# Second attention: both halves of a score tile ahead of the row chunks of their slot

## The chip, the core and the metric

The kernel runs on one core of a Trainium2 chip. TensorE (PE) multiplies, VectorE (DVE), ScalarE (ACT) and GpSimd (POOL) do the rest, and SyncE (SP) issues most DMAs. Each engine works through its own queue in order, and semaphores tie the queues together. The metric is the device time of one execution, in microseconds (us).

## What is computed

A two-layer transformer on x of shape (2, 1024, 256). Each layer is an attention and an MLP, each between layer norms with a residual sum: a 16-head attention in bf16, a mixture of 16 experts, then a "forgetting" attention with 32 heads of 8 in fp32, and an MLP with int8 weights. Only the forgetting attention is touched:

```python
q, k, v = heads of x @ Wq.T, x @ Wk.T, x @ Wv.T          # 32 heads of 8
c = cumsum(log_sigmoid(x @ Wf.T + bf), axis=1)
scores = einsum('bihd,bjhd->bhij', q, k) * scale + (c_i - c_j)
p = softmax(where(causal, scores, -inf))
o = einsum('bhij,bjhd->bihd', p, v) ; return o @ Wo.T
```

## The kernel before, in words

`attention` (L622) works through 32 units; a unit is two heads of one batch (1024 queries, 1024 keys). Each unit needs two passes of score matmuls.

The **row pass** finds the maximum of every query row. `row_chunk` (L680) multiplies a block of 128 queries with up to 512 keys into `row`, a ring of three PSUM buffers (`SLOTS`). DVE takes the maximum (`max_of`, L836: a masked custom operation at L845 for the last chunk of a row, a plain reduction at L849 otherwise) and frees the buffer (`row_free`). A unit has 24 chunks (`CHUNKS`, numbered 0 to 23). When all are through, `turn_max` (L691) transposes the maxima with eight small matmuls into one more `row` buffer, and DVE adds them to the rows of `q_sb` (`add_max`, L863). Chunks and turns are called entries; the entry n waits on PE until DVE has freed the entry n - 3.

The **score pass** makes the transposed, shifted scores. `scores(u, g, part)` (L708) issues one of the two halves of score tile g (two matmuls into `st`, a ring of two PSUM buffers); the second half fires `st_ready`. The first half waits until ACT has done the exp of tile g - 2. ACT does one exp per tile (L791 for the tiles 0 to 7 of one head, L794 for 8 to 11 of both), POOL clears what lies above the diagonal (L819), and `values` (L728) multiplies the probabilities with v into `o`. After the first exp of the next unit ACT copies `o` to `oT` (L779), which waits for the last values.

PE's order is written out by hand. The loop `for k in range(NGR)` has 12 slots a unit. Slot k issues the scores of tile k + 2 (in slots 10 and 11 the tiles 0 and 1 of the next unit), the row entries of `LATER[k]` for the next unit or the one after that, and in the odd slots the values of `VALUES[k]`. `LATER` is ((12, 13), (14, 15), (16, 17), (18, 19), (20, 21), (22, 23), (0, 1), (2,), (TURN, 3), (4, 5, 6), (7, 8, 9), (10, 11)). Before the change a slot is issued as: first half, first entry, second half, other entries, values. The last two units have no unit to prepare, so parts of their slots are empty.

Of the kernel before, what the change touches and what calls it, by code (L numbers as in the profile page):

```python
# [353 lines left out]
def columns_of(kb):  # L354


    at = [POS[qb] for qb in range(kb, TB)]
    return min(at) * P, (max(at) + 1) * P
# [18 lines left out]
def exp_groups():  # L377
# [10 lines left out]
LATER = ((12, 13), (14, 15), (16, 17), (18, 19), (20, 21), (22, 23),  # L388
         (0, 1), (2,), (TURN, 3), (4, 5, 6), (7, 8, 9), (10, 11))
# [232 lines left out]
def attention(nc, tag, units, hd, m_row, dt, load, k_steps, k_sb, v_units, o_rows, mask, ident_b):  # L622
# [11 lines left out]
    with ExitStack() as ctx:  # L634
# [19 lines left out]
        def columns(kb, h):  # L654


            lo, hi = columns_of(kb)
            return (lo, hi, 0) if kb < TB // 2 else (lo, hi, h * SIDE - lo)

        def group_of(kb, h):  # L660

            return 2 * kb + h if kb < TB // 2 else TB + kb - TB // 2

        @block.sync
        def _(sp):
            k_steps(sp, k_sb, steps_loaded)
            for u in range(RING):
                load(sp, u, q_sb[:, u], k_sb[:, u], qk_loaded[u])
            for u in range(units):
                if u and u + 3 < units:  # L670
                    sp.wait_ge(st_ready, NGR * u)
                    load(sp, u + 3, q_sb[:, (u + 3) % RING], k_sb[:, (u + 3) % RING], qk_loaded[(u + 3) % RING])
                sp.wait_ge(o_copied, u + 1)
                sp.dma_start(o_rows[u * 4 * HW:(u + 1) * 4 * HW, :], oT[:, u % 2]).then_inc(stored[u % 2], 16)
            for k in range(2):
                sp.wait_ge(stored[k], 16 * (units // 2))

        @block.tensor
        def _(pe):
            def row_chunk(u, i):  # L680

                qb, h, lo, w = CHUNKS[i]
                n = entry_of[u, i]
                if i == 0:
                    pe.wait_ge(qk_loaded[u % RING], 64 * (u // RING + 1))
                if n >= SLOTS:
                    pe.wait_ge(row_free, n - SLOTS + 1)
                nc.tensor.matmul(row[:, n % SLOTS, 0:w], q_sb[:, u % RING, POS[qb] * P:(POS[qb] + 1) * P],  # L688
                                 k_sb[:, u % RING, h, lo:lo + w], start=True, stop=True).then_inc(row_ready, 1)

            def turn_max(u):  # L691

                n = entry_of[u, TURN]
                pe.wait_ge(m_parts, 3 * (u + 1))
                pe.wait_ge(row_free, n - SLOTS + 1)
                turned = row[:, n % SLOTS].bitcast(BF16)
                for qb in range(TB):
                    last = nc.tensor.transpose(turned[:, POS[qb] * P:(POS[qb] + 1) * P],
                                               mcol[:, u % 2, qb].rearrange("p h r -> p (h r)"), ident_b[:])
                last.then_inc(row_ready, 1)  # L700

            def entry(u, what):
                if what == TURN:
                    turn_max(u)
                else:
                    row_chunk(u, what)

            def scores(u, g, part):  # L708

                kb, heads = GROUPS[g]  # L710
                n = NGR * u + g
                if part == 0:
                    if g == 0:

                        pe.wait_ge(row_free, entry_of[u, TURN] + 1)
                    if n >= 2:
                        pe.wait_ge(exp_done, n - 1)
                lo, hi = columns_of(kb)
                if len(heads) == 1:
                    h, first, end, to = heads[0], max(lo, SIDE * part), min(hi, SIDE * (part + 1)), 0  # L720
                else:
                    h, first, end, to = part, lo, hi, part * SIDE - lo
                last = nc.tensor.matmul(st[:, n % 2, to + first:to + end], k_sb[:, u % RING, h, kb * P:(kb + 1) * P],  # L723
                                        q_sb[:, u % RING, first:end], start=True, stop=True)
                if part == 1:
                    last.then_inc(st_ready, 1)

            def values(u, kb):  # L728

                if kb == 0:  # L730
                    pe.wait_ge(v_ready, u + 1)
                    if u:
                        pe.wait_ge(o_copied, u)
                pe.wait_ge(masked, TB * u + kb + 1)
                for side in range(2):
                    for h in range(2):
                        lo, hi, to = columns(kb, h)
                        first, end = max(lo, SIDE * side), min(hi, SIDE * (side + 1))
                        if first >= end:
                            continue  # L740
                        at = HW * (2 * h + side)
                        last = nc.tensor.matmul(o[at:at + HW, first - SIDE * side:end - SIDE * side],  # L742
                                                v_sb[:, u % RING, kb, h, :],
                                                probs[:, (NGR * u + group_of(kb, h)) % GR, to + first:to + end],
                                                start=(kb == 0), stop=(kb >= TB - 2), skip_group_check=True)
                last.then_inc(pv_done, 1)

            pe.wait_ge(steps_loaded, 32)
            for i in range(NC // 2):
                entry(0, i)  # L750
            for slot in LATER:
                for what in slot:
                    entry(0 if what == TURN or what >= NC // 2 else 1, what)
            for g in range(2):
                for part in range(2):
                    scores(0, g, part)

            for u in range(units):
                for k in range(NGR):
                    to_u, to_g = (u, k + 2) if k + 2 < NGR else (u + 1, k + 2 - NGR)  # L760
                    if to_u < units:
                        scores(to_u, to_g, 0)
                    for m, what in enumerate(LATER[k]):
                        to = u + 1 if what == TURN or what >= NC // 2 else u + 2
                        if to < units:
                            entry(to, what)
                        if m == 0 and to_u < units:
                            scores(to_u, to_g, 1)
                    for kb in VALUES.get(k, ()):
                        values(u, kb)  # L770

# [29 lines left out]
        @block.gpsimd  # L801
        def _(pool):
            def copy_v(u):
                if u >= RING:
                    pool.wait_ge(pv_done, TB * (u - RING + 1))
                nc.gpsimd.tensor_copy(v_sb[:, u % RING, :, :, 0:hd + 1], v_units[:, u]).then_inc(v_ready, 1)

            def causal(u, kb):

                n = NGR * u + group_of(kb, 1)  # L810
                pool.wait_ge(exp_done, n + 1)
                lo, _, _ = columns(kb, 0)
                if kb < TB // 2:
                    first = (n - 1) % GR
                    tiles = probs[:, first:first + 2, POS[kb] * P:(POS[kb] + 1) * P]
                else:
                    at = POS[kb] * P - lo
                    tiles = probs[:, n % GR].rearrange("p (h n) -> p h n", h=2)[:, :, at:at + P]
                nc.gpsimd.affine_select(tiles, tiles, [[0, 2], [1, P]], ALU.is_ge, 0.0, base=0,  # L819
                                        channel_multiplier=-1).then_inc(masked, 1)  # L820

            nc.gpsimd.memset(v_sb[:], 0.0).then_inc(v_clear, 1)
            pool.wait_ge(v_clear, 1)
            copy_v(0)
            for u in range(units):
                if u + 1 < units:
                    copy_v(u + 1)
                for kb in range(TB):
                    causal(u, kb)
# [964 lines left out]
```

## Time and profile before

| | |
|---|---|
| median of 3 runs | 1985.34 us (1984.33 to 1985.52) |
| profiled execution | 1983.64 us, span 1981.9 us |
| PE busy | 1522.3 us, 77% of the span |
| DVE busy | 1310.3 us, 66% |
| ACT busy | 844.9 us, 43% |
| POOL busy | 247.9 us, 13% |
| second attention | about 1221 to 1740 us of the span |

Times in rows are us from the span's start. A timeline row has the start, the length, the engine, the line, the operation, output <- inputs, the shape, and in brackets the idle time of the engine just ahead of it with what ended it. Matmul lengths overlap: what a matmul takes of PE is the distance to the next start. Rows of like instructions next to each other are merged ("x2"), and a few matmul records are missing.

### The profile page before, as it was taken

The numbers are of one execution on the slowest core, as the hardware profiler recorded it, in microseconds if no ns is written. First come the engines' busy times: TensorE is split into PE (matmuls) and PEld (weight loads), VectorE is DVE, ScalarE is ACT, GpSimd is POOL, SyncE is SP. The second block draws the span as 40 slices with busy tenths as digits, with TensorE's granted clock in tenths as the row PEclk, the third lists the DMA queues.
The fourth block names the chain that finished last, engine by engine and source line by source line (L and its number), as shares of the span: only waits on it lengthen the run. The fifth ranks groups of instructions, "written<-read, shape, count | busy, mean of one in ns | idle before, by whom it ended". The sixth has DMA issues, their size and how long they took to land. (4 is left out here: it accounts for less than half of the span.)

```text
span 1981.9 us, 28852 instructions
## 1 busy us (share of the span) xinstructions
PE 1522.3 (77%) x9011; PEld 827.1 (42%) x9088; DVE 1310.3 (66%) x3794; ACT 844.9 (43%) x1534; POOL 247.9 (13%) x409
## 2 busy tenths in 40 slices
PE   3555555542199999999999393999999999963995
PEld 1122222211167777777777261333333333341564
DVE  4888888866445554555455567888888888636543
ACT  3888988860011111111111240566666666623212
POOL 0000000000121121212110110222222222201000
PEclk9555555555599999999999695999999999976998
DMA  2255565651100000000000064111111111020001
GB/s 85 59 103 103 105 104 106 104 115 18 29 24 14 20 22 14 28 14 28 14 19 1 12 241 150 33 54 55 54 49 49 49 49 49 33 61 19 1 1 43
DMA packets 203881, 105.52 MB, mean 53 GB/s; under 512 B 164502, under 2 KB 180886, under 8 KB 203502
## 3 DMA queue, kind: packets, MB, share of 16 engines
q1 hardware_dynamic: 202542, 102.01, 20.8%
q10 hardware_dynamic: 1216, 2.03, 0.4%
q8 instruction: 57, 0.93, 0.2%
q14 instruction: 66, 0.54, 0.1%
HBM read 40.68 MB, written 29.36 MB: 35 GB/s over the span
## 5 line engine op out<-in xcount | busy, mean ns | idle before, releaser
L1221 PE MATMUL moe_gu<-all_xT_bf,moe_parts 128*112 128x512 bf16 x1536 | 344.9, 382 | 17.8 <-POOL moe_parts L1046 17.8
L1258 ACT ACTIVATE moe_th<-moe_gu 112x512 f32<-112x512 f32 x128 | 76.4, 597 | 489.2 <-PE moe_gu L1221 489.2
L791 ACT ACTIVATE a_probs<-a_st 128x1024 f32<-128x1024 f32 (+3 forms) x256 | 212.3, 865 | 158.4 <-PE a_st L723 158.3
L688 PE MATMUL a_row<-l_k,a_q 128*128 128x512 bf16 (+3 forms) x736 | 230.1, 334 | 45.4 <-DMA l_k<-k_rows 27.1
L1221 PEld LDWEIGHTS moe_gu<-all_xT_bf,moe_parts 128*112 128x112 bf16 x1536 | 201.2, 131 | 147.3 <-POOL moe_parts L1046 17.9
L845 DVE CUSTOM_DVE_ANT_0 a_unread<-a_row,all_mask 128x128 bf16<-128x128 f32 (+3 forms) x512 | 238.6, 485 | 32.2 <-PE a_row L688 27.6
L1274 DVE SCALAR_TENSOR_TENSOR moe_tmp<-moe_th,moe_gu 112x512 f32<-112x512 f32 x128 | 88.0, 687 | 255.4 <-ACT moe_th L1258 244.1
L723 PE MATMUL a_st<-a_q,l_k 128*128 128x384 bf16 (+3 forms) x735 | 223.6, 327 | 26.7 <-ACT a_probs L791 24.5
L1235 PE MATMUL moe_dn<-moe_wd,moe_actT 112*128 112x256 f32 x1024 | 231.4, 379 | 0.0
L570 DVE CUSTOM_DVE_ANT_0 a_rows<-a_sc,all_mask 128x128 bf16<-128x128 f32 (+7 forms) x256 | 192.5, 752 | 43.7 <-PE a_sc L493 42.5
L1235 PEld LDWEIGHTS moe_dn<-moe_wd,moe_actT 112*128 112x128 f32 x1024 | 194.7, 190 | 30.2
L849 DVE TENSOR_REDUCE a_mx<-a_row 128x1 f32<-128x512 f32 x256 | 175.9, 687 | 38.6 <-PE a_row L688 38.5
L506 PE MATMUL a_o<-a_v,a_turned_sb 128*128 128x16 bf16 x1152 | 73.6, 179 | 164.1 <-DMA a_turned_sb<-a_rows 163.5
L526 ACT ACTIVATE a_rows<-a_rows 128x128 bf16<-128x128 bf16 (+7 forms) x256 | 173.2, 677 | 40.9 <-DVE a_rows L580 35.9
L493 PE MATMUL a_sc<-a_k,a_q 16*128 16x512 bf16 (+3 forms) x384 | 167.5, 505 | 12.2 <-DVE a_mx L570 7.5
L742 PE MATMUL a_o<-a_probs,a_v 128*32 128x384 f32 (+3 forms) x1920 | 176.7, 432 | 0.0
L506 PEld LDWEIGHTS a_o<-a_v,a_turned_sb 128*128 128x128 bf16 x1152 | 50.6, 106 | 293.7 <-DMA a_turned_sb<-a_rows 265.7
L535 ACT ACTIVATE a_unread<-a_rows 128x128 bf16<-128x128 bf16 (+7 forms) x256 | 170.6, 666 | 0.0
L819 POOL TENSOR_SCALAR_AFFINE_SELECT a_probs<-a_probs 128x256 f32<-128x256 f32 x256 | 102.5, 406 | 412.1 <-ACT a_probs L791 336.1
L723 PEld LDWEIGHTS a_st<-a_q,l_k 128*128 128x128 bf16 x768 | 73.7, 97 | 184.1 <-ACT a_probs L791 112.5
L688 PEld LDWEIGHTS a_row<-l_k,a_q 128*128 128x128 bf16 x768 | 75.1, 98 | 124.1 <-DVE a_mx L849 31.8
L1288 DVE SCALAR_TENSOR_TENSOR all_y<-moe_dn,moe_wcur,all_y 128x256 f32<-128x256 f32 x256 | 111.7, 477 | 15.5 <-PE moe_dn L1235 15.5
(198 smaller groups left out, 1668.1 us busy)
## 6 DMA issues: line engine op xcount, KB each, us to landing
a_q<-q_rows SPq DMA_DIRECT2D x64, 128.0 KB
l_k<-k_rows SPq DMA_DIRECT2D x64, 128.0 KB
o_rows<-a_oT SPq DMA_DIRECT2D x32, 256.0 KB, 2.0
a_turned_sb<-a_rows SPq DMA_TRANSPOSE x256, 2.6
moe_raw<-in_gate SPq DMA_DIRECT2D x16, 224.0 KB, 3.1
moe_raw<-in_up SPq DMA_DIRECT2D x16, 224.0 KB, 3.4
moe_wd<-in_down SPq DMA_DIRECT2D x16, 224.0 KB, 2.8
q_rows<-qkv_parts SPq DMA_DIRECT2D x4, 768.0 KB, 3.6
```

Of the source, the lines that this page charges most:

```text
L493: last = nc.tensor.matmul(sc[:, n % 3, lo // 512, 0:w], q_sb[32 * h:32 * h + hd, u % 2, qb * P:(qb + 1) * P], k_sb[32 * h:32 * h + hd, u % ...
L526: nc.scalar.activation(row, row, ACT.Exp).then_inc(exp_done, 1)
L535: nc.scalar.activation(unread[:, n % 2, 0:w], rows[:, u % 2, at:at + w], ACT.Copy, accum_out=total[:, u % 2, e:e + 1]).then_inc(summed, 1)
L570: nc.vector.tensor_tensor_reduce(out=rows[:, u % 2, at:at + w], in0=sc[:, n % 3].rearrange("p a n -> p (a n)")[:, 0:w], in1=mask[:, S - w: ...
L688: nc.tensor.matmul(row[:, n % SLOTS, 0:w], q_sb[:, u % RING, POS[qb] * P:(POS[qb] + 1) * P], k_sb[:, u % RING, h, lo:lo + w], start=True, ...
L723: last = nc.tensor.matmul(st[:, n % 2, to + first:to + end], k_sb[:, u % RING, h, kb * P:(kb + 1) * P], q_sb[:, u % RING, first:end], star ...
L742: last = nc.tensor.matmul(o[at:at + HW, first - SIDE * side:end - SIDE * side], v_sb[:, u % RING, kb, h, :], probs[:, (NGR * u + group_of( ...
L791: nc.scalar.activation(probs[:, n % GR, lo:hi], st[:, n % 2, lo:hi], ACT.Exp).then_inc(exp_done, 1)
L845: nc.vector.tensor_tensor_reduce(out=unread[:, n % SLOTS, 0:w], in0=tile[:, 0:w], in1=mask[:, at:at + w], scale=1.0, scalar=-3e38, op0=ALU ...
L849: nc.vector.tensor_reduce(top, tile[:, 0:w], mybir.AxisListType.X, ALU.max).then_inc(row_free, 1)
L1221: last = nc.tensor.matmul(gu[0:IC, n % 2, i, :], parts[:, j, k // KC, i, k % KC, ch * IC:(ch + 1) * IC], xT[:, k % KC, g * 512:(g + 1) * 512],
L1235: last = nc.tensor.matmul(dn[:, i, 0:D], actT[:, g % 2, ch, i * P:(i + 1) * P], wd[:, j, ch, :], start=(ch == 0), stop=(ch == 1))
```

## The change

In each slot the second half of the score tile is issued straight behind the first half, ahead of all row entries. What is issued in a slot, and how often, stays the same, and so do the other engines' queues and all waits.

```diff
                     to_u, to_g = (u, k + 2) if k + 2 < NGR else (u + 1, k + 2 - NGR)
                     if to_u < units:
                         scores(to_u, to_g, 0)
-                    for m, what in enumerate(LATER[k]):
+                        scores(to_u, to_g, 1)
+                    for what in LATER[k]:
                         to = u + 1 if what == TURN or what >= NC // 2 else u + 2
                         if to < units:
                             entry(to, what)
-                        if m == 0 and to_u < units:
-                            scores(to_u, to_g, 1)
                     for kb in VALUES.get(k, ()):
                         values(u, kb)
```

## Rows read from the trace of the kernel before

**Rows 1.** Windows: length, busy PE, PEld, DVE, ACT, POOL; PEclk, DMA, GB/s.

```profile
1400.00:1500.00 100.00, 91.45 (x714) 35.83 (x727) 82.66 (x275) 61.97 (x83) 22.05 (x57) 1.00 0.17 56
...
1728.00:1740.00 12.00, 9.79 (x92) 3.15 (x92) 0.00 (x0) 9.73 (x14) 3.20 (x8) 1.00 0.07 25
1740.00:1750.00 10.00, 0.23 (x1) 0.27 (x2) 3.73 (x2) 0.00 (x0) 0.00 (x0) 0.58 0.70 176
```

**Rows 2.** Waits, 1250 to 1730 us: us in total, times, longest.

```profile
PEld a_st L723 <- ACT a_probs L791: 104.7, 121, 1.2
...
ACT a_oT L779 <- PE a_o L742: 28.2, 30, 0.9
PEld a_row L688 <- DVE a_mx L849: 26.3, 60, 0.5
PE a_st L723 <- ACT a_probs L791: 22.5, 30, 0.8
```

**Rows 3.** Timeline of PE, slots 8 and 9 of one unit.

```profile
1266.70 0.61 PE L698 MATMUL a_row<-all_ident_b,a_mcol 128*128 128x128 bf16 x8
1267.15 0.27 PE L723 MATMUL a_st<-a_q,l_k 128*128 128x256 bf16 x1
1267.26 0.22 PE L688 MATMUL a_row<-l_k,a_q 128*128 128x128 bf16 x1
...
1268.10 0.50 PE L688 MATMUL a_row<-l_k,a_q 128*128 128x512 bf16 x2 [0.29 <-DVE a_q L866]
```

**Rows 4.** Timeline of PE and its weight loads (PEld), slots 10 and 11 of the same unit.

```profile
1269.96 0.38 PE L723 MATMUL a_st<-a_q,l_k 128*128 128x512 bf16 x1
1270.18 0.43 PE L688 MATMUL a_row<-l_k,a_q 128*128 128x384 bf16 x2
...
1270.90 0.10 PEld L688 LDWEIGHTS a_row<-l_k,a_q 128*128 128x128 bf16 x1 [0.47 <-DVE a_mx L849]
1270.91 0.39 PE L688 MATMUL a_row<-l_k,a_q 128*128 128x512 bf16 x1 [0.30 <-DVE a_mx L849]
...
1271.38 0.34 PE L688 MATMUL a_row<-l_k,a_q 128*128 128x384 bf16 x1
```

**Rows 5.** Timeline of PE, end of slot 0 and start of slot 1.

```profile
1272.78 0.38 PE L688 MATMUL a_row<-l_k,a_q 128*128 128x512 bf16 x1
1273.91 0.39 PE L723 MATMUL a_st<-a_q,l_k 128*128 128x512 bf16 x1 [0.75 <-ACT a_probs L791]
```

**Rows 6.** Timeline of DVE, the same slots.

```profile
1267.35 0.69 DVE L866 TENSOR_TENSOR a_q<-a_row,a_q 128x1024 bf16<-128x1024 bf16 x1 [0.51 <-PE a_row L698]
...
1270.16 0.69 DVE L849 TENSOR_REDUCE a_mx<-a_row 128x1 f32<-128x512 f32 x1 [0.36 <-PE a_row L688]
...
1271.24 0.08 DVE L845 DVE_READ_ACCUMULATOR2_ANT a_mx<- 128x1 f32 x1
...
1276.25 0.69 DVE L849 TENSOR_REDUCE a_mx<-a_row 128x1 f32<-128x512 f32 x1 [0.90 <-PE a_row L688]
```

**Rows 7.** Timeline of ACT: copies of o 15 units apart, and the exps behind.

```profile
1272.34 0.58 ACT L779 COPY a_oT<-a_o 128x512 f32<-128x512 f32 x1 [0.94 <-PE a_o L742]
1272.82 2.70 ACT L791 ACTIVATE a_probs<-a_st 128x1024 f32<-128x1024 f32 x3
...
1509.74 0.58 ACT L779 COPY a_oT<-a_o 128x512 f32<-128x512 f32 x1 [0.94 <-PE a_o L742]
```

**Rows 8.** Timeline of PE, slots 2 and 3.

```profile
1276.05 0.33 PE L723 MATMUL a_st<-a_q,l_k 128*128 128x384 bf16 x1
1276.21 0.27 PE L688 MATMUL a_row<-l_k,a_q 128*128 128x256 bf16 x1
...
1277.00 0.39 PE L688 MATMUL a_row<-l_k,a_q 128*128 128x512 bf16 x1
```

**Rows 9.** Timeline of DVE and PE, slots 4 and 5: chunks 20 and 23.

```profile
1278.89 0.08 DVE L845 DVE_READ_ACCUMULATOR2_ANT a_mx<- 128x1 f32 x1
...
1279.34 0.22 PE L688 MATMUL a_row<-l_k,a_q 128*128 128x128 bf16 x1
```

## Prediction

> **What bounds the kernel now.** I read the windows first. In the second attention TensorE (PE) is busy 91 of 100 us, DVE 83, ACT 62, at a granted clock of 1.00 [rows 1]. No engine is full, so the waits come next, then the order of instructions in one unit.
>
> The table of waits [rows 2] misleads at its top: the loads for `a_st` (L723) sat idle 104.7 us "for ACT". A load row is idle while the values' matmuls run ahead of it on PE. Of PE proper only 22.5 us, 30 times, waited for ACT, and loads of row chunks waited 26.3 us, 60 times (two a unit), for DVE's reductions.
>
> So I laid out one unit. The copies of `o` to `oT` stand at 1272.34 and 1509.74, 15 units apart: 15.83 us a unit [rows 7]. In these 15.83 us PE's queue, which goes strictly in program order, is stopped at five places. "Chunk i" is entry i of `CHUNKS`, "slot k" one pass of `for k in range(NGR)`.
> 1. Slot 9, chunk 5: waits until DVE has read the turned maxima (`add_max`, L866), since it takes the same `row` buffer. DVE's 1267.35 + 0.69 = 1268.04, PE goes at 1268.10 [rows 3, 6].
> 2. Slot 11, chunk 10: waits for chunk 7's reduction, 1270.16 + 0.69 = 1270.85, PE goes at 1270.91 [rows 4, 6].
> 3. Slot 11, chunk 11: waits for chunk 8, read out at 1271.24 + 0.08 = 1271.32, PE goes at 1271.38 [rows 4, 6].
> 4. Slot 1, first half of group 3: waits for the exp of group 1, which ends about 1.03 after 1272.82; PE goes at 1273.91, against a queue free at 1272.78 + 0.22 = 1273.00: 0.91 us [rows 5].
> 5. Slot 3, chunk 19: waits for chunk 16's reduction, 1276.25 + 0.69 = 1276.94, PE goes at 1277.00 [rows 6, 8].
>
> A release thus costs 0.06 us each time. Everything else is PE issuing without a stop. Wait 4 isn't about scores: group 1's exp starts at 1272.82 because ACT was in the copy of `o` from 1272.34, and the copy had waited for the last values [rows 2, 7], which stand behind chunk 11 on PE. So the unit is one ring of PE issue, PE to DVE to PE hand-offs (1, 2, 3, 5) and one hand-off by way of values, copy and exp (4).
>
> **The change part by part.** No instruction is added or removed, and no DMA, SP or POOL instruction is moved. In each slot the second half of a score tile goes ahead of the slot's first row entry. (a) The second half comes earlier by the first entry's time. (b) The first entry comes later by the second half's time. Later entries and values stay where they were in the queue.
>
> (a) **What comes earlier.** `st_ready` fires 0.06 us (one matmul of 128 columns) to 0.45 us (the turn) sooner [rows 3], so 12 exps a unit can start sooner. PE waits for an exp only at place 4, and that exp starts behind the copy of `o`, not behind its scores: its second half is issued soon after 1270.91, over a microsecond before 1272.82 [rows 4, 7]. The other scores go when the values ahead of them are through. Gain: 0. The earlier exps are paid out as ACT idle time. If this cover were gone, the gain could be wait 4 at most, 0.91 us a unit.
>
> (b) **What comes later.** In nine of twelve slots the delayed chunk is one that nobody waits for: PE reads no `row` result, DVE has a backlog or idle time, and the chunk three entries on is far behind. It decides where a later chunk already waits for DVE's release of it. Those are the places above:
> - Slot 8 holds the turn of the maxima. Its eight transposes go at 1266.70, ahead of the second half of group 10 (256 columns). That half takes 1267.15 to 1267.26 = 0.11 us of PE [rows 3]. Afterwards it is ahead, the turn ends 0.11 later, `add_max` starts 0.11 later (DVE was idle 0.51 us for exactly this [rows 6]), and chunk 5 goes 0.11 later: **+0.11**.
> - Slot 10, chunk 7: the second half (512 columns) takes 1269.96 to 1270.18 = 0.22 us [rows 4]. DVE was idle 0.36 us for chunk 7 [rows 6], so its reduction slips by 0.22. The releases for chunks 10 and 11 slip with it (DVE runs 7, 8, 9 back to back). In slot 11 both halves now go first and then PE stands twice: chunk 10 goes at 1270.91 + 0.33, chunk 11 at 1271.38 + 0.33 (0.33 with the 0.11 of the turn). The values and the copy behind chunk 11, and so wait 4, follow: **+0.22**.
> - Slot 2, chunk 16: the second half (384 columns) takes 1276.05 to 1276.21 = 0.16 us [rows 8]. DVE had been idle 0.90 us for chunk 16 [rows 6]; it and the release for chunk 19 slip. The values of slot 3 stand behind chunk 19: **+0.16**.
> - The next tightest is chunk 23 in slot 5, which needs chunk 20: DVE has read chunk 20 at 1278.89 + 0.08 and 0.06 later is 1279.03, against chunk 23 at 1279.34: 0.31 us to spare, 0.15 after chunk 20's delay by 0.16 (its slot's second half has 384 columns too) [rows 9]. No wait; if that slack were wrong, at most 0.16 more a unit.
>
> The three add, since each shifts the whole ring and no slack lies between: wait 4 moves with the copy, and the table of waits has no line in which PE's values wait for POOL. **0.11 + 0.22 + 0.16 = 0.49 us a unit**, 15.83 to 16.32. The first two happen in the units 0 to 29 (in the last two no chunk follows), the third in 0 to 30: 30 x 0.33 + 31 x 0.16 = 14.9 us.
>
> The profiled execution has 1983.64 us (span 1981.9). 1983.64 + 14.9 = 1998.5, that is +0.75%. It lies 1.7 below the median of the runs, 1985.34, so I add the same there: **2000.2 us**.
>
> Bounds of the unknown. The order "half, half, chunk" has no row in this trace. Nearest are the eight transposes: eight loads and matmuls of 128 columns fit in 1266.70 to 1267.15, 0.056 each [rows 3], so a load hides behind even the shortest matmul: extra cost 0. The far bound is one load of 0.10 us [rows 4] exposed per unit where a wait moved, 3 us in all. Below: one of the three slips absorbed by a slack that I missed, minus 3 to 6 us. I take the sum as it is.
>
> **The rivals.**
> - *Earlier scores pay* (faster). If the exp that PE waits for were released by its scores, the whole wait 4 (0.91 us) could shrink by what the second half of slot 11 moves forward, about 0.47 us a unit, 31 times: -14 us, 1971. For it: the waits table puts PE's waits for ACT first [rows 2]. Against: group 1's exp starts straight after the copy [rows 7]. It decides only if the copy stopped being the releaser.
> - *Nothing happens.* The delayed chunks vanish in DVE's idle time (17 of 100 us [rows 1]): 1985. Against: the idle time lies exactly ahead of the instructions that are delayed [rows 6].
> - *Partly absorbed.* One or two of the three terms count: +5 to +10 us, 1990 to 1995.
> - *A fourth wait*, chunk 23 or exposed loads: 2003 to 2005.
> - *The clock falls.* PE now stands 0.49 us a unit more. The granted clock was 1.00 at 91% busy and still 1.00 in 1728 to 1740 at 82%; it was down only in 1740 to 1750, where PE did almost nothing [rows 1]. I compute 91.45 x 15.83/16.32 = 88.7 busy afterwards, above that 82. A unit at the lower level (1.2 GHz) would take up to some 14 us more, its PE issue time again (15.83 less the stops, an estimate); three units of 32 would give 2042. The Trainium skill has the rule against this change ("TensorE: Matmul & The Clock Gate", section "A second HAM failure mode: psum-queue depth-cycling"): frequent micro-idles between groups of matmuls can make the clock swing between its levels. By that rule the stage would lose tens of us; this trace doesn't bear it out, with its five stops a unit at 1.00 throughout.
>
> **How the numbers follow.** Forecast 0.74, earlier scores pay 0.05, nothing 0.08, partly absorbed 0.08, a fourth wait 0.03, clock 0.02. The range 1994 to 2005 takes in the forecast with its bounds (2000.2 minus one term of 5, plus 0.16 x 31 = 5), the upper part of the partly absorbed case and the fourth wait: about 0.8. Some 0.2% (4 us) is what a measurement of this kernel can tell from no change. Faster 0.05; same 0.08; slower 0.87.
>
> **What would show it.** Period of the copies 16.32 us in place of 15.83. Stage longer by 14.9 us, all else unchanged. Idle of DVE per unit up by 0.49: ahead of `add_max` 0.51 to about 0.62, ahead of chunk 7 0.36 to about 0.58, ahead of chunk 16 0.90 to about 1.06. PE's stops at chunk 10 and chunk 11 both about 0.25 us, at chunk 19 0.14 to 0.30; wait 4 unchanged at 0.91. Exps relative to PE earlier, and ACT's idle time total up by 0.49 a unit all the same. Busy share of PE 89 of 100 us and clock still 1.00. I'd be wrong if DVE's idle gaps grew but the period didn't, if wait 4 shrank, or if a load row stood exposed between the halves.

## The result, and the profile after

The changed kernel takes 2001.32 us (median of 4 runs, 2000.48 to 2002.54) against 1985.43 us: ratio 1.0080, interval 1.0063 to 1.0098, 15.9 us slower. The profiled execution has a span of 1999.1 us against 1981.9. Two single executions of kernels tried below lie far outside all others, one with slot 10 alone (3753.36 us) and one with nine slots (2291.72 us); nothing explains them, and times and ratios leave them out.

First the copies of `o` to `oT` on ACT, as in [rows 7]; these two are 14 units apart.

```profile
1276.47 0.58 ACT L778 COPY a_oT<-a_o 128x512 f32<-128x512 f32 x1 [1.37 <-PE a_o L742]
...
1504.88 0.58 ACT L778 COPY a_oT<-a_o 128x512 f32<-128x512 f32 x1 [1.37 <-PE a_o L742]
```

(1504.88 - 1276.47) / 14 = 16.315, so 16.32 us a unit, as forecast, where it was 15.83. (The lines of the file have moved up by one: L778 is the L779 of before.) ACT stood 1.37 us ahead of the copy in place of 0.94: the exp of the next group 0 was earlier, the values later. ACT got its scores sooner and spent the gain waiting.

PE's timeline of one unit at its stops. 1272.02 (chunks 5 and 6) answers to [rows 3], 1275.05 (chunks 10 and 11) to [rows 4], 1278.04 (both halves of group 3) to [rows 5], 1280.78 (chunks 18 and 19) to [rows 8]:

```profile
1271.24 0.38 PE L688 MATMUL a_row<-l_k,a_q 128*128 128x512 bf16 x1
1272.02 0.50 PE L688 MATMUL a_row<-l_k,a_q 128*128 128x512 bf16 x2 [0.40 <-DVE a_q L865]
...
1274.37 0.38 PE L723 MATMUL a_st<-a_q,l_k 128*128 128x512 bf16 x1
1275.05 0.81 PE L688 MATMUL a_row<-l_k,a_q 128*128 128x512 bf16 x2 [0.30 <-DVE a_mx L848]
...
1276.75 0.54 PE L688 MATMUL a_row<-l_k,a_q 128*128 128x384 bf16 x2
1278.04 0.55 PE L723 MATMUL a_st<-a_q,l_k 128*128 128x512 bf16 x2 [0.75 <-ACT a_probs L790]
1278.43 0.43 PE L688 MATMUL a_row<-l_k,a_q 128*128 128x256 bf16 x2
...
1280.45 0.49 PE L723 MATMUL a_st<-a_q,l_k 128*128 128x384 bf16 x2
1280.78 0.90 PE L688 MATMUL a_row<-l_k,a_q 128*128 128x512 bf16 x2
```

Chunk 5 is stopped with 0.40 idle where it was 0.29. Chunk 10 stands about 0.24: the two halves ahead of it (the record of the second is missing) take 0.22 each from 1274.37, so the queue is free at 1274.81. The pair of chunks 10 and 11 spans 0.81 us; without a stop between them it would be 0.22 + 0.33 = 0.55, so chunk 11 stands about 0.25 as well. The pair of 18 and 19 spans 0.90 where two 512-column chunks in a row take 0.22 + 0.38 = 0.60: chunk 19 stands 0.30, before 0.14. The wait for the exp of group 1 has kept its 0.75 of idle time. Counted from the queue being free, as the prediction counts it, it is 1278.04 - (1276.75 + 0.16 + 0.22) = 0.91, also as before.

DVE in the same unit, as [rows 6]:

```profile
1271.27 0.69 DVE L865 TENSOR_TENSOR a_q<-a_row,a_q 128x1024 bf16<-128x1024 bf16 x1 [0.62 <-PE a_row L698]
...
1274.30 0.69 DVE L848 TENSOR_REDUCE a_mx<-a_row 128x1 f32<-128x512 f32 x1 [0.58 <-PE a_row L688]
...
1277.11 0.56 DVE L844 CUSTOM_DVE_ANT_0 a_unread<-a_row,all_mask 128x384 bf16<-128x384 f32 x1 [0.23 <-PE a_row L688]
...
1280.55 0.69 DVE L848 TENSOR_REDUCE a_mx<-a_row 128x1 f32<-128x512 f32 x1 [0.90 <-PE a_row L688]
```

The idle time ahead of `add_max` grew from 0.51 to 0.62 and ahead of chunk 7 from 0.36 to 0.58. Ahead of chunk 16 it is still 0.90, and there is a new 0.23 ahead of chunk 12 (below).

The waits from 1250 to 1745 us, as [rows 2], and the window that answers to [rows 1]. The first line here is of the kernel before (its waits from 1250 to 1730 us), for the last line of the next fence:

```profile
PE a_row L688 <- DVE a_q L866: 8.8, 30, 0.3
```

```profile
PEld a_st L723 <- ACT a_probs L790: 105.8, 122, 1.2
...
ACT a_oT L778 <- PE a_o L742: 41.2, 30, 1.4
...
PEld a_row L688 <- DVE a_mx L848: 34.5, 60, 0.6
...
PE a_st L723 <- ACT a_probs L790: 22.5, 30, 0.8
...
PE a_row L688 <- DVE a_q L865: 12.1, 30, 0.4
```

```profile
1400.00:1500.00 100.00, 89.98 (x707) 35.88 (x718) 79.98 (x268) 59.93 (x82) 21.98 (x57) 1.00 0.15 48
```

PE's real wait for ACT is 22.5 us before and after. What grew are the waits for DVE: PE's own for `add_max` from 8.8 to 12.1 us (30 x 0.11), and that of the row chunks' loads for DVE's reductions from 26.3 to 34.5. (The latter are load rows, so they show which wait grew and not by how much PE stood.) PE, DVE, ACT and POOL are all less busy, and the granted clock is still 1.00.

### The profile page after: what moved, and what is told of

The parts are those of the page before. It is cut to its first block and busy times, and to the rows that moved or that the text cites. A ratio compares the mean times of both kernels' runs of the same rounds, so it can differ in the third digit from the quotient of the medians.

```text
span 1999.1 us, 28852 instructions
## 1 busy us (share of the span) xinstructions
PE 1528.7 (76%) x9011; PEld 828.1 (41%) x9088; DVE 1307.5 (65%) x3794; ACT 842.9 (42%) x1534; POOL 249.0 (12%) x409
## 5 line engine op out<-in xcount | busy, mean ns | idle before, releaser
L790 ACT ACTIVATE a_probs<-a_st 128x1024 f32<-128x1024 f32 (+3 forms) x256 | 207.6, 867 | 171.3 <-PE a_st L723 171.2
L688 PE MATMUL a_row<-l_k,a_q 128*128 128x512 bf16 (+3 forms) x735 | 201.9, 334 | 50.6 <-DMA l_k<-k_rows 26.9
L723 PE MATMUL a_st<-a_q,l_k 128*128 128x384 bf16 (+3 forms) x736 | 183.4, 329 | 30.9 <-ACT a_probs L790 23.9
L723 PEld LDWEIGHTS a_st<-a_q,l_k 128*128 128x128 bf16 x768 | 55.7, 98 | 166.9 <-ACT a_probs L790 112.5
L1287 DVE SCALAR_TENSOR_TENSOR all_y<-moe_dn,moe_wcur,all_y 128x256 f32<-128x256 f32 x256 | 111.7, 477 | 15.6 <-PE moe_dn L1234 15.5
```

The source lines that it names most:

```text
L790: nc.scalar.activation(probs[:, n % GR, lo:hi], st[:, n % 2, lo:hi], ACT.Exp).then_inc(exp_done, 1)
```

## The experiments

Each is shown with its edit, what was expected of it and the period of a unit from two copies in its trace. The slot sets below are tested in one loop; `TOGETHER` and `CHUNK_FIRST` stand for the sets, which each kernel has written into that line. Unless another set is named, both are empty, which is the order of before:

```diff
+                    together, chunk_first = k in TOGETHER, k in CHUNK_FIRST
-                    if to_u < units:
+                    if to_u < units and not chunk_first:
                         scores(to_u, to_g, 0)
+                        if together:
+                            scores(to_u, to_g, 1)
                     for m, what in enumerate(LATER[k]):
...
-                        if m == 0 and to_u < units:
+                        if m == 0 and to_u < units and chunk_first:
+                            scores(to_u, to_g, 0)
+                        if m == 0 and to_u < units and not together:
                             scores(to_u, to_g, 1)
```

### One slot at a time

Slot 8 alone (`TOGETHER = (8,)`):

> The kernel before, with both halves first in slot 8 alone (the slot of the turn). Theory of three hand-offs: the turn, add_max and chunk 5 go 0.11 us later, nothing else: period of a unit 15.83 + 0.11 = 15.94 us, 30 x 0.11 = +3.3 us. Rival, a small cost in every slot (0.49 / 12 = 0.04 us each, from pairing the halves): period 15.87, +1.3 us. Rival, no effect of this slot (DVE's idle time takes it): 15.83, 0.

```profile
1274.26 0.58 ACT L784 COPY a_oT<-a_o 128x512 f32<-128x512 f32 x1 [0.94 <-PE a_o L742]
...
1513.31 0.58 ACT L784 COPY a_oT<-a_o 128x512 f32<-128x512 f32 x1 [0.94 <-PE a_o L742]
```

239.05 / 15 = 15.94 us. Time 1988.28 against 1985.01, ratio 1.0018 (1.0009 to 1.0028), +3.3 us.

Slot 10 alone (`TOGETHER = (10,)`):

> The kernel before, with both halves first in slot 10 alone (chunk 7). Three hand-offs: chunk 7 goes 0.22 us later, and with it the releases for chunks 10 and 11 and all that follows: period 16.04 us, 30 x 0.22 = +6.5 us. Cost in every slot alike: 15.87, +1.3 us. No effect: 15.83, 0.

```profile
1272.08 0.59 ACT L784 COPY a_oT<-a_o 128x512 f32<-128x512 f32 x1 [1.37 <-PE a_o L742]
...
1512.70 0.59 ACT L784 COPY a_oT<-a_o 128x512 f32<-128x512 f32 x1 [1.37 <-PE a_o L742]
```

240.62 / 15 = 16.04 us. Time 1992.07, ratio 1.0040 (1.0024 to 1.0056), +7.1 us.

Slot 2 alone (`TOGETHER = (2,)`):

> The kernel before, with both halves first in slot 2 alone (chunk 16). Three hand-offs: chunk 16 and the release for chunk 19 go 0.16 us later: period 15.99 us, 31 x 0.16 = +5.1 us. Cost in every slot alike: 15.87, +1.3 us. No effect: 15.83, 0.

```profile
1273.32 0.59 ACT L784 COPY a_oT<-a_o 128x512 f32<-128x512 f32 x1 [0.94 <-PE a_o L742]
...
1513.17 0.59 ACT L784 COPY a_oT<-a_o 128x512 f32<-128x512 f32 x1 [0.94 <-PE a_o L742]
```

239.85 / 15 = 15.99 us. Time 1989.27, ratio 1.0020 (1.0008 to 1.0031), +4.3 us.

The other nine slots (`TOGETHER` = all but 2, 8 and 10):

> The changed kernel with the slots 2, 8 and 10 put back to the old order: both halves first in the nine others. Three hand-offs: period 15.83 us and the time of the kernel before, within 0.1%. Cost in every slot alike: 9 x 0.04 = 0.37 us a unit more, period 16.19, +11 us. Earlier scores pay: below 15.83.

```profile
1274.35 0.58 ACT L784 COPY a_oT<-a_o 128x512 f32<-128x512 f32 x1 [0.94 <-PE a_o L742]
...
1511.77 0.59 ACT L784 COPY a_oT<-a_o 128x512 f32<-128x512 f32 x1 [0.94 <-PE a_o L742]
```

237.42 / 15 = 15.83 us. Time 1986.71, +1.7 us, ratio 1.0007 (0.9997 to 1.0017): no difference clear of noise. The three slots' excess over 15.83 is 0.11 + 0.21 + 0.16 = 0.48 us a unit, the whole change's 0.49, the other nine's 0. So the cost isn't one of pairing the halves, or of loading weights twice in a row; it sits in three slots, in the sizes of the second halves that were put ahead there. DVE in the kernel with the nine slots:

```profile
1274.99 0.56 DVE L850 CUSTOM_DVE_ANT_0 a_unread<-a_row,all_mask 128x384 bf16<-128x384 f32 x1 [0.23 <-PE a_row L688]
...
1278.26 0.69 DVE L854 TENSOR_REDUCE a_mx<-a_row 128x1 f32<-128x512 f32 x1 [0.73 <-PE a_row L688]
```

It stands 0.23 us ahead of chunk 12, which slot 0's second half made late, and makes up for it ahead of chunk 16: 0.73 in place of 0.90. In this kernel the delay is free, since DVE's next idle time takes it up and no stop of PE depends on it in between.

### The wait for the exp of group 1

ACT's copy goes behind the exp of group 1:

```diff
-                    if g == 0 and u:
+                    if g == 1 and u:
                         copy_out(u - 1)
```

> The kernel before, with ACT's copy of o to oT moved from behind the exp of group 0 to behind that of group 1. It takes wait 4 (0.91 us a unit) out of the ring, if that wait was due to the copy and not to the scores. Theory: exp of group 1 starts as its scores are there, PE doesn't stop in slot 1: period 15.83 - 0.91 = 14.92 us, 31 x 0.91 = -28 us. Rival, the scores released that exp: 15.83, 0.

```profile
1269.93 0.58 ACT L784 COPY a_oT<-a_o 128x512 f32<-128x512 f32 x1
...
1508.38 0.58 ACT L784 COPY a_oT<-a_o 128x512 f32<-128x512 f32 x1
```

238.45 / 16 = 14.90 us. Time 1955.61 against 1985.54, ratio 0.9852 (0.9836 to 0.9869), -29.9 us. Nothing about the scores was changed, and 0.93 us a unit went. So the biggest stop of PE was due to the copy, not to late scores.

The same with both halves first in all slots:

> The copy moved as in the other run, and both halves first in every slot as in the changed kernel. Three hand-offs: they cost the same 0.49 us without wait 4: period 14.92 + 0.49 = 15.41 us, 15 us slower than with the moved copy alone. Rival, earlier scores pay once the copy isn't the releaser: as fast as the moved copy alone or faster, 14.92 or below. Rival, wait 4 was needed for the loss to show: the loss shrinks to under 0.3 us a unit.

```profile
1273.42 0.58 ACT L784 COPY a_oT<-a_o 128x512 f32<-128x512 f32 x1 [0.46 <-PE a_o L742]
...
1506.25 0.58 ACT L784 COPY a_oT<-a_o 128x512 f32<-128x512 f32 x1 [0.45 <-PE a_o L742]
```

232.83 / 15 = 15.52 us. Time 1975.35, ratio 0.9949 (0.9932 to 0.9965). Earlier scores don't pay here either; the loss is 0.62 us a unit and 19.7 us in all, more than the 0.49 that I expected. The further 0.13 can be found in the trace. Chunks 14 and 15 in PE's timeline, and DVE's reading of chunk 12:

```profile
1507.28 0.57 PE L688 MATMUL a_row<-l_k,a_q 128*128 128x256 bf16 x2
```

```profile
1506.89 0.56 DVE L850 CUSTOM_DVE_ANT_0 a_unread<-a_row,all_mask 128x384 bf16<-128x384 f32 x1 [0.23 <-PE a_row L688]
1507.37 0.08 DVE L850 DVE_READ_ACCUMULATOR2_ANT a_mx<- 128x1 f32 x1
```

The pair takes 0.57 us where the changed kernel has 0.43 (1278.43 above): chunk 15 waits for chunk 12, free at 1507.45 plus 0.06. With the copy moved alone, chunk 12 was read at 1509.29 and chunk 15 went at 1509.39, so it had 0.04 us to spare after the 0.06, and slot 0's 0.16 is more than that. With the wait for the exp gone, nothing lies any more between slot 0, which delays chunk 12, and chunk 15. That stop had been a cover for slot 0's delay: one of the "nine free slots" costs 0.13 us as soon as it is taken away. This is read from the trace; slot 0 alone with the moved copy was not run.

### The other direction

Entries first, then both halves, in the three slots (`TOGETHER = ()`, `CHUNK_FIRST = (2, 8, 10)`):

> The opposite of the change in its three deciding slots: in the slots 2, 8 and 10 the first entry goes ahead of both halves, the other slots as in the kernel before. Three hand-offs: chunk 7 comes 0.22 us sooner, the turn 0.11, chunk 16 0.16 of which only the wait of 0.14 at chunk 19 can be won: period 15.83 - 0.47 = 15.36 us, -14 us. Rival, the old order was at its optimum (later scores now stop ACT and PE): 15.83 or above.

```profile
1274.93 0.59 ACT L784 COPY a_oT<-a_o 128x512 f32<-128x512 f32 x1 [0.72 <-PE a_o L742]
...
1505.26 0.59 ACT L784 COPY a_oT<-a_o 128x512 f32<-128x512 f32 x1 [0.72 <-PE a_o L742]
```

230.33 / 15 = 15.36 us, 0.47 below 15.83 as expected. Time 1969.91 against 1985.54, ratio 0.9921 (0.9905 to 0.9938), -15.6 us: the mirror of the change, at the three places that decide.

With the moved copy as well:

> Moved copy and entries first in the slots 2, 8 and 10. If both gains are of one ring they add: period 15.83 - 0.91 - 0.47 = 14.45 us, -43 us, some 1942 us. If DVE (busy 13.2 us a unit) or ACT becomes the bound in places, less: up to 14.9 us.

```profile
1272.43 0.58 ACT L784 COPY a_oT<-a_o 128x512 f32<-128x512 f32 x1
...
1503.29 0.58 ACT L784 COPY a_oT<-a_o 128x512 f32<-128x512 f32 x1
```

230.86 / 16 = 14.43 us. Time 1943.15, ratio 0.9792 (0.9775 to 0.9808). The two gains add: 15.83 - 0.93 - 0.47 = 14.43.

Then the turn one slot earlier, so that chunk 5 needn't wait for `add_max`. Slot 8 no longer holds the turn and goes back to the old order, `CHUNK_FIRST = (2, 10)`:

```diff
-         (0, 1), (2,), (TURN, 3), (4, 5, 6), (7, 8, 9), (10, 11))
+         (0, 1), (2, TURN), (3,), (4, 5, 6), (7, 8, 9), (10, 11))
```

> Moved copy, entries first in the slots 2 and 10, and the turn of the maxima one slot earlier (end of slot 7, ahead of the values, in place of the start of slot 8). With the moved copy and entries first in 2, 8 and 10 the one stop of PE left is chunk 5's wait for add_max, about 0.34 us a unit (1513.56 against a queue free at 1513.16 + 0.06). Theory: the turn comes early enough, the stop is gone: period 14.43 - 0.34 = 14.09 us, -10 us against that kernel, about 1933 us. Rival, DVE (13.2 us of work a unit) becomes the bound or the turn then waits for the parts of the maximum: 14.4 or above.

```profile
1273.45 0.58 ACT L784 COPY a_oT<-a_o 128x512 f32<-128x512 f32 x1
...
1499.72 0.58 ACT L784 COPY a_oT<-a_o 128x512 f32<-128x512 f32 x1
```

```profile
1400.00:1500.00 100.00, 98.52 (x813) 41.38 (x828) 93.13 (x311) 68.41 (x93) 24.41 (x64) 1.00 0.17 56
```

226.27 / 16 = 14.14 us. Time 1934.27 against 1985.43, ratio 0.9740 (0.9723 to 0.9756): 51 us below the kernel before, and the fastest of all. PE is busy 98.5 of 100 us, DVE 93.1; the stage is bound by PE now. The period is 0.05 us above the 14.09 expected. Chunk 2 and the second half behind it, and the turn:

```profile
1507.33 0.38 PE L688 MATMUL a_row<-l_k,a_q 128*128 128x512 bf16 x1
1507.55 0.33 PE L723 MATMUL a_st<-a_q,l_k 128*128 128x384 bf16 x1
1507.78 0.61 PE L698 MATMUL a_row<-all_ident_b,a_mcol 128*128 128x128 bf16 x8
```

A half of 384 columns takes 0.16 us, so the turn could start at 1507.71 and starts 0.07 later. It has two waits, for the parts of the maximum and for its `row` buffer. In the trace both were met in time: DVE's last part ended at 1507.44, and it had read chunk 0, whose buffer the turn takes, at 1507.63, which with the usual 0.06 makes 1507.69. What holds the turn is open.

The earlier turn in the changed kernel alone:

> The changed kernel (both halves first in every slot) with the turn one slot earlier. If the turn's term of 0.11 us exists only because chunk 5 waits for add_max, it goes with the whole stop: 1272.02 against a queue free at 1271.24 + 0.22, 0.56 us: period 16.32 - 0.56 = 15.76 us, -17 us against the changed kernel, about 1984 us, with the terms of chunks 7 and 16 still in it. Rival, other stops take its place: above 15.9.

```profile
1274.02 0.58 ACT L778 COPY a_oT<-a_o 128x512 f32<-128x512 f32 x1 [1.37 <-PE a_o L742]
...
1511.52 0.58 ACT L778 COPY a_oT<-a_o 128x512 f32<-128x512 f32 x1 [1.37 <-PE a_o L742]
```

237.5 / 15 = 15.83 us, 0.48 below the changed kernel, where I expected 0.56. Time 1986.14 against 1985.43, ratio 1.0005 (0.9995 to 1.0014). The stop at chunk 5 is gone, and 0.07 came back at the turn:

```profile
1267.33 0.38 PE L688 MATMUL a_row<-l_k,a_q 128*128 128x512 bf16 x1
...
1267.59 0.46 PEld L698 LDWEIGHTS a_row<-all_ident_b,a_mcol 128*128 128x128 bf16 x8 [0.32 <-DVE a_mcol L859]
1267.62 0.61 PE L698 MATMUL a_row<-all_ident_b,a_mcol 128*128 128x128 bf16 x8
```

Chunk 2 at 1267.33 takes 0.22 us; the turn goes at 1267.62, not 1267.55. The bracket names DVE's parts of the maximum, but these were done at 1267.28, and chunk 0 was read at 1267.47. So here too neither wait explains the 0.07.

## Why the prediction was right, point by point

- **Direction and size.** Forecast 2000.2 us, measured 2001.3; +14.9 against +15.9. The period 16.32 was met to 0.01 us.
- **The three terms.** 0.11, 0.22 and 0.16 a unit were forecast. One slot at a time gave 0.11, 0.21 and 0.16, and the other nine gave nothing. Their place was right too: `add_max` idle 0.62 and chunk 7 idle 0.58, as forecast; chunk 10's and 11's stops both about 0.25 and chunk 19's 0.30.
- **The gain of 0.** The second halves came sooner and ACT began sooner, and PE's wait for the exp of group 1 stayed at 0.75 idle in the trace. The moved copy shows why: that exp had been held by the copy. The rival "earlier scores pay" was to decide once the copy isn't the releaser. With the copy moved, the halves-first order loses 0.62 a unit, so the rival fails there as well.
- **One detail wrong.** I put the new idle time of DVE ahead of chunk 16 (0.90 to 1.06). It came ahead of chunk 12 (0.23), and chunk 16 kept its 0.90: slot 0's own second half, which has 384 columns too, had already made DVE 0.16 us late for the chunks 12 to 15. Chunk 16 then came 0.16 late as well, so the idle time between them stayed as long. The price of the step stands, since PE's release for chunk 19 follows chunk 16's arrival, and that was 0.16 later. The step that in nine of twelve slots nobody waits for the delayed chunk was right for this kernel and too general: it was true of slot 0 only under the cover of the wait for the exp.
- **The clock.** Granted was 1.00 from 1400 to 1500, as before, with PE busy 90 of 100 us and with longer stops. The rival that the clock falls had no part, and the rule of the Trainium skill ("TensorE: Matmul & The Clock Gate", "A second HAM failure mode: psum-queue depth-cycling") isn't seen in this pattern.
- **The missing microsecond.** The profiled executions differ by 17.2 us, more than the 14.9. From the first copy to the last, the stage took 482.90 us before (1256.51 to 1739.41) and 497.21 after (1260.16 to 1757.37). That is 14.31 more, and with 0.49 for the unit ahead of the first copy the new order makes 14.8 us, as forecast. The rest lies at the two ends. The first matmul of the stage, before:

```profile
1221.27 0.26 PE L688 MATMUL a_row<-l_k,a_q 128*128 128x128 bf16 x1 [27.15 <-DMA l_k<-k_rows]
```

and after:

```profile
1222.69 0.26 PE L688 MATMUL a_row<-l_k,a_q 128*128 128x128 bf16 x1 [26.94 <-DMA l_k<-k_rows]
```

So 1.42 us were there before anything that the change touches had run; in the kernel with the nine slots, which has the period of before, the same matmul stands at 1223.01. From it to the first copy the changed kernel took 37.47 us against 35.24: 0.49 by the order, and 1.74 more. In these microseconds the granted clock was lower. The windows 1239 to 1246 of before, of the nine slots and of after:

```profile
1239.00:1246.00 7.00, 6.12 (x33) 2.11 (x37) 4.89 (x18) 4.85 (x6) 0.82 (x2) 0.94 0.00 0
```

```profile
1239.00:1246.00 7.00, 6.35 (x25) 1.67 (x24) 5.14 (x18) 3.56 (x4) 0.52 (x2) 0.74 0.00 0
```

```profile
1239.00:1246.00 7.00, 6.31 (x20) 2.02 (x24) 4.39 (x16) 3.37 (x4) 0.42 (x1) 0.50 0.00 0
```

The granted clock was 0.94, 0.74 and 0.50. What PE issues ahead of this stretch is the same in all three kernels. The changed kernel with the earlier turn, which also has both halves first everywhere, had 0.70 there and lost only 0.36 us up to the first copy (1222.59 to 1258.19), so I take the late clock for a difference between executions. Behind the last copy the changed kernel was 0.76 us quicker: 1.42 + 1.74 + 14.8 - 0.76 = 17.2. That the median's further 1 us (15.9 against 14.9) is such a difference too is likely and not shown.

## What to carry to other kernels

In a pipeline of engines that hand buffers round, list the places where the bounding engine's queue stands, and for each the one instruction that releases it. Here an instruction put ahead of the work that feeds such a release cost its own length in full, however idle the engines looked, and handing work earlier to an engine that nobody waited for paid nothing. Where a stop lies between the delayed work and the next wait for it, the delay is hidden until that stop is removed. Check each stop for its real releaser before buying it off: here it was a copy that stood between two exps, and moving it (one character) brought 30 us, while the reordering for ACT's sake cost 16.

## What the runs showed of the hardware

Two score halves in a row, with a load of 128 columns for each, cost no more than a half and a chunk in turn: with nine such slots the period was that of before to 0.01 us. A stop can hide the cost of an order: with the wait for the exp removed, the same order cost 0.62 us a unit in place of 0.49. PE's granted clock was 1.00 in the windows of 100 us both at 90% busy and at 98.5%. The 0.07 us at the earlier turn I had not expected, and its cause is open.
